# First attention of a decoder layer: written out by key group, value products of 512 columns, output copies ahead of the probability copies

## The reference

```python
q = qkv[..., :QPG * D].reshape(b, s, NKV, QPG, D)      # QPG = 4 query heads to a key head
k = qkv[..., QPG * D:(QPG + 1) * D]
v = qkv[..., (QPG + 1) * D:]
scores = jnp.einsum('bsgqd,btgd->bgqst', q, k) * scale
scores = jnp.where(causal, scores, jnp.finfo(scores.dtype).min)
attn = jax.nn.softmax(scores, axis=-1)
out = jnp.einsum('bgqst,btgd->bsgqd', attn, v)
return jnp.einsum('bse,he->bsh', out.reshape(b, s, NH * D), weight_proj)

x = x + _L0_attn_ref(_layernorm(x, axis=-1), L0_attn_weight_qkv, L0_attn_weight_proj)
```

## Time and profile before

| | |
|---|---|
| device time, three runs | 1064.21, 1069.08, 1064.57 us; median 1064.57 |
| the profiled execution's own time | 1061.68 us |
| its span, first to last instruction | 1059.8 us |
| busy, TensorE / its weight loads | 898.9 / 775.7 us |
| busy, VectorE / ScalarE / POOL | 563.2 / 435.0 / 260.3 us |
| mean granted clock of TensorE | 0.940 of 2.4 GHz |

### The profile page before, as it was taken

One profiled execution on the slowest core, in us unless ns is written; L12 is line 12 of the kernel. 1 busy time (PEld: TensorE's weight loads), 2 busy tenths in 40 slices (PEclk: granted clock), 3 DMA queues, 4 the chain that ended last, 5 costly groups with the idle time before them and its releaser, 6 DMA issues. The chain is left out here.

```text
span 1059.8 us, 17723 instructions
## 1 busy us (share of the span) xinstructions
PE 898.9 (85%) x5670; PEld 775.7 (73%) x5671; DVE 563.2 (53%) x1593; ACT 435.0 (41%) x1102; POOL 260.3 (25%) x448
## 2 busy tenths in 40 slices
PE   4799988999899999997878979796661799999990
PEld 3699977998799988997758567583631588888880
DVE  5755645565465655565484746556379223333225
ACT  4465635655466545663343323243061222222220
POOL 0233202322133212322011110101121344444430
PEclk9899999999999999999898989899875799999995
DMA  9100000000000000000160240707094111111117
GB/s 349 60 2 1 2 4 2 1 2 1 4 2 1 2 1 2 2 1 21 60 141 19 65 93 0 158 0 158 21 377 158 30 54 50 54 49 49 49 42 245
DMA packets 45596, 61.85 MB, mean 58 GB/s; under 512 B 3472, under 2 KB 36368, under 8 KB 45392
## 3 DMA queue, kind: packets, MB, share of 16 engines
q1 hardware_dynamic: 39664, 48.58, 15.9%
q0 software_dynamic: 3744, 10.23, 3.1%
q10 hardware_dynamic: 2112, 2.10, 0.6%
HBM read 34.81 MB, written 9.31 MB: 42 GB/s over the span
## 5 line engine op out<-in xcount | busy, mean ns | idle before, releaser
L246 POOL TENSOR_TENSOR prob<-prob,rinv 128x128 f32<-128x128 f32 (+1 forms) x256 | 124.5, 508 | 329.6 <-DVE rinv L312 329.6
L286 ACT ACTIVATE prob<-masked,negmax 128x128 f32<-128x128 f32 (+1 forms) x256 | 114.6, 448 | 182.4 <-DVE negmax L375 182.4
L301 DVE TENSOR_TENSOR pT_lo<-bank_t,pT_hi 128x384 fp32r<-128x384 f32 x128 | 70.7, 553 | 60.3 <-ACT pT_hi L258 60.3
L301 DVE TENSOR_TENSOR qT_lo<-bank_q,qT_hi 128x512 fp32r<-128x512 f32 x64 | 44.2, 691 | 94.4 <-ACT qT_hi L258 94.4
L38 PE MATMUL bank_s<-kT_hi,qT_hi 128*128 128x128 f32 (+1 forms) x256 | 78.1, 305 | 10.5 <-DVE WprojT_lo L332 6.5
L1444 DVE TENSOR_TENSOR f_xT_lo<-bank_o,f_xT_hi 128x256 fp32r<-128x256 f32 x39 | 16.6, 425 | 128.2 <-ACT f_xT_hi L1291 128.2
L375 DVE CUSTOM_DVE_ANT_0 masked<-bank_s,causal 128x128 f32<-128x128 f32 (+1 forms) x256 | 79.0, 346 | 0.0
L38 PE MATMUL bank_o<-pT_hi,v_hi 128*128 128x256 f32 (+1 forms) x256 | 74.9, 293 | 0.5 <-DVE pT_lo L301 0.5
L1589 PE MATMUL bank_y<-f_Wo,f_interT 128*128 x312 | 73.9, 380 | 0.8 <-ACT f_interT L1286 0.8
L38 PE MATMUL bank_y<-WprojT_hi,oT_hi 128*128 128x256 f32 x256 | 72.3, 282 | 0.0
L39 PE MATMUL bank_y<-WprojT_lo,oT_hi 128*128 128x256 f32 x256 | 71.9, 281 | 0.0
(11 more groups left out here) (276 smaller groups left out, 2518.8 us busy)
## 6 DMA issues: line engine op xcount, KB each, us to landing
b_VW_hi<-b_VWs_hi SPq DMA_DIRECT2D x32, 256.0 KB, 4.7
b_VW_lo<-b_VWs_lo SPq DMA_DIRECT2D x32, 256.0 KB, 4.8
f_W_lo<-in_L_ffn_w_kernel_dram SPq DMA_DIRECT2D x16, 512.0 KB, 9.7
f_Wo<-in_L_ffn_wo_kernel_dram SPq DMA_DIRECT2D x8, 512.0 KB, 9.3
stage<-n_L_attn_weight_qkv_dram SPq DMA_DIRECT2D x6, 512.0 KB, 7.7
stage<-_L_attn_weight_proj_dram SPq DMA_DIRECT2D x4, 512.0 KB, 10.8
WqT<-in_L_xattn_Wq_dram SPq DMA_DIRECT2D x1, 2048.0 KB, 20.0
b_wo<-in_L_xattn_Wo_dram SPq DMA_DIRECT2D x1, 2048.0 KB, 8.8
```

Of the source, the lines that this page charges most:

```text
L246: pool.tensor_tensor(prob[:, u % 3, a:b], prob[:, u % 3, a:b], rinv[:, u % 4, i:i + 1].to_broadcast([P, b - a]), ALU.mult)\
L286: act.activation(prob[:, s % 3, a:b], masked[:, s % 2, a:b], ACT.Exp, scale=-1.0, bias=negmax[:, s % 4, i:i + 1], accum_out=rowsum[:, s % ...
L301: dve.tensor_tensor(dst.lo, src, dst.hi.bitcast(F32), ALU.subtract).then_inc(free[n], 1)
```

## The change

The first attention is written out in full: no loop over passes, one sequence of 128 + 8 steps in which the pipeline isn't emptied between passes. What differs:

- **Order of the units.** By key group: the four query heads of a key head for the first sequence, then for the second. `qT` holds four heads.
- **Value products.** Four units share key tiles, so their transposed probabilities stand side by side (`pT` is 128 x 3 x 4 x 128) and `values` makes nine matmuls of 512 columns every fourth step: three into o0 (queries of the first half) and six into o1 (second half, two key tiles).
- **Copies.** In step s ScalarE takes: exponential of s, the fill's copy, both output copies if the step has value products, then the probability copy of unit s-2. VectorE: reciprocal of s-1, masked scores of s, then the low halves in the same order.
- **Projection.** One head of one sequence at a time (six matmuls), four steps in a row behind the value products.
- **Fills.** All in bank q. Queries of the next group, keys, values and the next pass's transposes are spread over the steps. A bank y has one residual for each pass, taken while the next pass runs.
- **Head.** Only three weight pieces are split ahead of the steps; the other seven stand at the ends of steps 0 to 12. Statistics and normalisation of the next pass stand at the ends of steps 11 to 21 of a pass.
- **Loads.** The second attention's query weights, context and mask are loaded when all splits are done, its key weights when the last transposes are made, its value weights at the start of its own block.

```diff
-                vg = v[:, :, g * D:(g + 1) * D]
-                mm3(pe, bank[n][:, b * S:b * S + S], vg[:, 2 * b, :], pT[:, u % 2, 0:S], True, False)
-                ins = mm3(pe, bank[n][:, b * S + P:b * S + S], vg[:, 2 * b + 1, :], pT[:, u % 2, S:CW],
-                          False, True)
+        def values(G):
+            p, g, b, _ = unit(G * QPG)
+            copied(("t", G * QPG + QPG - 1))
...
+            vg = v[:, :, g * D:(g + 1) * D]
+            wait_free(("o", G, 0))
+            mm3(pe, bank["o0"][:], vg[:, 2 * b, :], pT[:, 0, :, :].view("p h q -> p (h q)"), True, True)\
+                .then_inc(full["o0"], 1)
+            wait_free(("o", G, 1))
+            mm3(pe, bank["o1"][:], vg[:, 2 * b, :], pT[:, 1, :, :].view("p h q -> p (h q)"), True, False)
+            mm3(pe, bank["o1"][:], vg[:, 2 * b + 1, :], pT[:, 2, :, :].view("p h q -> p (h q)"), False, True)\
+                .then_inc(full["o1"], 1)
```

The steps on TensorE, and the fills by step (`pv_at`, `proj_at` and `t_at` give the group or unit whose products, projection and transposes stand in step s: s-6 every fourth step, s-7, and s-2):

```diff
+        within = {0: ("v", 0), 2: ("v", 1), 3: ("v", 2), 5: ("v", 3), 8: ("k", 2), 10: ("k", 3)}
+        ahead = {-6: ("xt", 0), -5: ("k", 0), -4: ("q", 0, 0), -3: ("k", 1), -2: ("q", 0, 1), -1: ("q", 0, 2),
+                 1: ("q", 0, 3)}
+        for g in range(1, NKV):
+            for i, at in enumerate((-4, -2, -1, 1)):
+                within[8 * g + at] = ("q", g, i)
...
+                for s in range(STEPS):
+                    if s in waits:
+                        pe.wait_ge(w_lo, PIECES.index(waits[s]) + 1)
+                    if s < ALL:
+                        scores(s)
+                    proj_now = proj_at(s)
+                    if proj_now and proj_now[1] == QPG - 1:
+                        project(*proj_now)
+                    name = fill_at(s)
+                    if name:
...
+                        fill(name)
+                    if pv_at(s) is not None:
+                        values(pv_at(s))
+                    if t_at(s) is not None:
+                        transposes(t_at(s))
+                    if proj_now and proj_now[1] < QPG - 1:
+                        project(*proj_now)
```

And on ScalarE:

```diff
+                for s in range(STEPS):
+                    if s < ALL:
+                        act.wait_ge(masked_ready, 2 * (s + 1))
+                        if s >= 3:
+                            act.wait_ge(full["t"], banks.count(("t", s - 3)))
+                        for i, (a, b) in enumerate(((0, P), (P, CW))):
+                            act.activation(prob[:, s % 3, a:b], masked[:, s % 2, a:b], ACT.Exp, scale=-1.0,
...
+                    if fill_at(s):
+                        high(fill_at(s))
+                    if pv_at(s) is not None:
+                        high(("o", pv_at(s), 0))
+                        high(("o", pv_at(s), 1))
+                    if t_at(s) is not None:
+                        high(("t", t_at(s)))
+                    if s in split_at:
+                        split_hi(split_at[s])
+                    if late_fill_at(s):
+                        high(late_fill_at(s))
```

More of the change, by code:

```diff
@@ new lines, in high, with split_hi @@
+                    if len(dst.hi.shape) == 3:
+                        src = src.rearrange("p (a b) -> p a b", a=dst.hi.shape[1])
+                    act.wait_ge(full[n], banks.count(name))
+                    act.activation(dst.hi, src, ACT.Copy).then_inc(half[n], 1)
+                def split_hi(n):
+                    act.wait_ge(w_loaded[n], 16)
+                    act.activation(part[n].hi, staged[n], ACT.Copy).then_inc(w_hi, 1)
+                split_hi("k")
+                high(first[0][0])
@@ new lines, in _ @@
+                low(first[0][0])
+                low(first[1][0])
+                split_lo("q0")
+                low(first[2][0])
+                low(first[3][0])
+                split_lo("v")
+                for name, _ in first[4:]:
+                    low(name)
+                dve.wait_ge(mask_made, 3)
+                for s in range(STEPS):
+                    p, r = divmod(s, UNITS)
+                    if 1 <= s <= ALL:
+                        invert(s - 1)
+                    if s < ALL:
+                        n = banks.bank(("s", s))
+                        dve.wait_ge(full[n], banks.count(("s", s)))
@@ L404, in fill, with copied @@
[L404 to L408 removed]
+                    before = banks.uses[n][count - 2]
+                    if before[0] == "s":
+                        pe.wait_ge(masked_ready, 2 * (before[1] + 1))
+                    else:
+                        pe.wait_ge(free[n], count - 1)
+                def copied(name):
+                    n, count = banks.at[name]
+                    pe.wait_ge(free[n], count)
@@ new lines, in project @@
+                def project(G, i):
+                    p, g, b, _ = unit(G * QPG)
+                    y = bank[("y0", "y1")[b]]
+                    if i == 0:
+                        copied(("o", G, 0))
+                        copied(("o", G, 1))
+                        if g == 0 and p > 0:
+                            pe.wait_ge(x_updated[b], p)
+                    h = QPG * g + i
+                    for t in range(2):
+                        ins = mm3(pe, y[:, t * HID:(t + 1) * HID], oT[:, i, t, :], WprojT[:, h, :],
+                                  h == 0 and t == 0, h == NH - 1)
+                    if h == NH - 1:
+                        ins.then_inc(y_full[b], 1)
```

524 lines of the change are left out of this document (244 added, 280 removed).

## The result

The changed kernel takes 1077.32 us (median of four runs, 1075.74 to 1077.61), the kernel before 1065.21 in the same rounds (1064.21 to 1069.08). The ratio is 1.0104, 95% interval 1.0076 to 1.0131: about 12 us slower. Forecast were 1072 us, in a range of 1044 to 1090, with 0.57 for slower.

What follows compares the result with a forecast made beforehand. The prediction took the turn between ScalarE and VectorE, not TensorE, to bound the changed kernel: 22.8 + 125 + 2 x 119.0 + 121.2 = 507.0 us against 500.0, so +7.0, 1068.7 profiled, 1072 forecast, range 1044 to 1090.

Steps and rivals of the forecast that it cites:

- The ring: First attention: masked scores, exponential, ScalarE's copies, VectorE's low copies, next masked scores; 27.1 us per eight units against TensorE's 23.8.
- the other signs named ahead: First attention: eight units in 27 us, TensorE waiting some 60 us, first masked scores at 23, last residual near 507.
- Product steps: Steps with value products: 4.1 us without a fill, 5.3 with a query fill, the second output copy awaiting all nine products.
- One pass: A middle pass of the first attention: 119.0 us, from four cycles at 108.4 plus fills, transposes and layer norm.
- The head: Work before the first masked scores: ends at about 22.8 us, 12.9 earlier than the 35.7 before.
- the split price: Seven weight splits inside the first pass's steps lengthen them by 1.4 us each, 10 us in all.
- The first pass: First pass of the first attention: 125 us, with 10 added by splits and about 4 given back by its first steps.
- The last pass: Last pass of the first attention: 121.2 us, with a serial tail of 10.6 behind the last masked scores.
- the 110.6 for the steps: Last pass without its tail: 119.0 less the next pass's fills, transposes and normalisation.
- First rival: First attention: TensorE stays the bound as output copies cost no more than before; about 1014 us, chance 0.13.
- Second: Value-product steps cost only 3.3 and 4.5 us instead of 4.1 and 5.3; about 1047 us, chance 0.12.
- Third: TensorE's clock falls once in each of sixteen cycles, through waits from 1.85 us on; +26, about 1098 us, chance 0.12.

Runs made afterwards that it cites:

- The first run: Kernel before, with ScalarE's high output copy moved behind the exponential and ahead of the probability copy in odd steps; 1096.97 us against 1065.96, ratio 1.028.
- The run with halves: Changed kernel with each 512-column value product written as two of 256 columns; 1076.13 us.

## Why the prediction was right

- **The ring, not TensorE, sets the steps.** Forecast 2.6, 3.3, 4.1 and 5.3; measured in the last pass 2.60, 3.30, 4.23 and 5.46, eight units 27.39 against 27.1. The first run confirms it in the kernel before, by order alone; in the changed kernel the runs without output copies and with both the copies and the first projection deferred do. Of the other signs named ahead, TensorE's waits came to 50 us of some 60. One thing the prediction did not see: with key and value fills in the steps TensorE is nearly full as well, so there both limits lie close together.
- **Product steps were sized short,** by 0.13 to 0.16, and by up to 0.6 behind a step with a fill. The timeline of all engines in a product step without a fill:

```profile
484.57 0.27 DVE L413 CUSTOM_DVE_ANT_0 masked<-bank_s,causal 128x128 f32<-128x128 f32 x1
484.63 0.50 PE L38 MATMUL bank_o<-pT_hi,v_hi 128*128 128x512 f32 x1
...
484.97 0.39 PE L39 MATMUL bank_o<-pT_lo,v_hi 128*128 128x512 f32 x1
...
487.02 0.60 ACT L307 ACTIVATE oT_hi<-bank_o 128x512 fp32r<-128x512 f32 x1 [0.33 <-PE bank_o L40]
```

  The products start 0.06 after the masked scores, as forecast, but the second matmul follows the first by 0.34 and not 0.23, and the second high copy starts 2.45 after the masked scores instead of 2.3. Product steps with a key or value fill, two a pass, were sized at 5.1 and take 5.67. So do the two of the four with a query fill that follow a step with a fill (5.66 to 5.69 against 5.3), since TensorE's work from the step before then lies in front of the products too. In a middle pass the eight product steps are 1.7 us over their sizes, and the other steps, layer norm among them, 0.7 under.
- **One pass** 119.0, measured 120.0 twice. **The head** 22.8, measured 22.89; the split price of 10 us measured 9.6, or 7.7 at a higher clock. **The first pass** 125, measured 127.6; without the splits it takes 118.0 where my terms give 115. It has 1.0 from the longer pass, and what its first steps lack (probability copies, products) gives back 2.0 us and not the 4 of the prediction.
- **The last pass was the largest miss:** 121.2, measured 514.63 - 390.58 = 124.05. From the last masked scores, at 500.84, to the last residual's end it takes 13.8 us where the prediction has 10.6. TensorE's transposes and the first product there:

```profile
501.00 0.52 PE L494 MATMUL bank_t<-ident,prob 128*128 128x128 f32 x3 [0.95 <-DVE pT_lo L352]
...
503.59 0.52 PE L494 MATMUL bank_t<-ident,prob 128*128 128x128 f32 x3 [1.38 <-DVE pT_lo L352]
...
505.37 0.52 PE L494 MATMUL bank_t<-ident,prob 128*128 128x128 f32 x3 [0.57 <-DVE pT_lo L352]
...
507.10 0.46 PE L38 MATMUL bank_o<-pT_hi,v_hi 128*128 128x512 f32 x1
```

  Behind the last masked scores stand three rounds of transposes and their copies, 2.6, 1.8 and 1.7 us, where the prediction has two for 3.3; the products and output copies (3.8 against 3.6), the projections (3.0 against 2.9) and the residual came as sized. The first round belongs to the last step, which the 110.6 for the steps may be taken to hold. Then the tail is 11.2 against 10.6, and the steps are 112.9 against 110.6, for the product steps above.
- **The total came closer than its parts, by luck.** The stage ended 14.6 us later instead of 7.0. The profiled execution came to 1077.4 against 1068.7, 8.7 off; the median missed the forecast by only 5.3, since the profiled execution of the kernel before, from which I worked, lay 3.5 below its median here and the forecast added 2.9, while that of the changed kernel lay at its median.
- **First rival** (TensorE stays the bound, 1014) is out by the stretches. The rule of the Trainium skill ("Perfetto Trace Analysis", section Identifying the Most-Contended Engine) stands behind it. As to what bounds the kernel before, the trace agrees: TensorE is never idle in the earlier trace rows. What doesn't follow is that less of its work makes the kernel faster: weight loads fell from 28.52 to 22.02 in 30 us, and the time rose. **Second** (cheap product steps, 1047): out; they cost more than I walked. **Third** (the clock, 1098): out from 120 us on, where the granted clock is 1.00; but TensorE's longest wait there is 1.5 us, less than the 1.85 from which this rival was to decide, so its condition was never met. The Trainium skill ("TensorE: Matmul & The Clock Gate", section "A second HAM failure mode: psum-queue depth-cycling") tells of a kernel whose clock oscillated by short, frequent idles; no stretch between 120 and 510 us shows that here, in spite of the waits. From 30 to 120 us, with waits of up to 2.0 us, the clock was 0.85, 0.98 and 0.94. The run with halves has the same waits there and 0.94, 1.00 and 1.00, and its first pass takes 125.8 us instead of 127.6. So some 1.8 of the 2.6 us by which the first pass missed go with the clock.

## What to carry to other kernels

When several in-order engines hand one item around, add up the latency of one turn, position by position, beside the busy shares: work that saves time on the fullest engine is worth nothing once the turn is longer. Copies whose source comes late in a step belong behind what the next turn needs, on each engine, and their first user must be moved as well, or the wait reappears in front of whatever stands behind that user. Undo the parts of a combined change one by one: here unrolling gained 9 us while the rest of the change cost 20.

## What the runs showed of the hardware

- Value products of 256 and of 512 columns cost the same per column: 18 and 9 matmuls take 2.17 and 2.21 us, and the kernels 1076.13 and 1077.32 us.
- Straight-line code for all passes ran no slower than the loop: 1057.34 against 1066.8 in the same rounds. Its five runs scatter 2.5 us where the sixteen of the loop scatter 8; other straight-line kernels here scatter from 0.6 to 12 us, so the scatter isn't the loop's alone.
- The same waits of TensorE, up to 2.0 us, went with a granted clock of 0.85, 0.98, 0.94 in one kernel's profiled execution and of 0.94, 1.00, 1.00 in that of the run with halves; the first pass took 127.6 and 125.8 us.
